# Second batch's first normalised x turned by transfers and VectorE block transposes; another order where the feed-forward begins; the last tile in two banks

## The reference, cut to what matters

```python
mod = (silu(c) @ wmod).reshape(2, 6, 1, -1)      # sa, ca, ga, sb, cb, gb
ga, gb = sign(g) * max(|g|, 0.25)                # for both gates
h = layernorm(x) * (1 + ca) + sa
x = x + ga * (h @ (weight * block_mask).T)       # 512 x 512, mask in 32 x 32 blocks
h = layernorm(x) * (1 + cb) + sb
inner = silu((h @ Wg.T) * ag) * ((h @ Wu.T) * au)   # 1376 wide
x = x + gb * ((inner @ Wd.T) * ad)
```

## Time and profile before

| | us |
|---|---|
| median of three runs | 180.3 |
| profiled execution, its own time | 180.65 |
| its span, first to last instruction | 178.5 |
| PE busy in the span | 170.8 |
| ACT, DVE, POOL busy | 82.0, 95.1, 29.6 |
| transfers | 22.93 MB |

### The profile page before, as it was taken

The page is one execution under the profiler, slowest core; times in us unless marked ns, Lnnn a source line. Parts: engine busy times, 40 slices in busy tenths (PEclk is TensorE's granted clock), DMA queues, the critical chain, the costliest instruction groups (busy, mean ns, idle before and its releaser), DMA issues.

```text
span 178.5 us, 2520 instructions
## 1 busy us (share of the span) xinstructions
PE 170.8 (96%) x893; PEld 129.6 (73%) x893; DVE 95.1 (53%) x194; ACT 82.0 (46%) x115; POOL 29.6 (17%) x40
## 2 busy tenths in 40 slices
PE   6979999999999999999999999999999999999990
PEld 6945545665458688788888888888888888888870
DVE  6882661483285798345455764327644223444493
ACT  3022213717979986833664444543335534242200
POOL 1443420292009330000000000005500000000000
PEclk9999999999999999999999999999999999999999
DMA  5999998999208700441300000001500000000033
GB/s 174 362 410 394 421 410 310 407 409 400 80 2 268 221 0 14 101 98 31 121 0 4 6 0 0 4 0 39 194 9 0 4 0 4 0 6 0 0 118 121
DMA packets 11668, 22.93 MB, mean 128 GB/s; under 512 B 2712, under 2 KB 4768, under 8 KB 11136
## 3 DMA queue, kind: packets, MB, share of 16 engines
q1 hardware_dynamic: 10528, 21.57, 33.3%
q10 hardware_dynamic: 1120, 1.07, 1.8%
HBM read 19.48 MB, written 2.10 MB: 121 GB/s over the span
## 4 chain that ended last, share of the span: by engine, by line
PE 86%; ACT 4%; DVE 3%; DMA 3%; issue 2%; SPq 1%; ACTq 0%
PE bank L771 45%; PE bank L825 23%; PE bank L741 12%; PE bank L685 3%; ACT junk L385 3%; PE bank L725 3%; DMA xt<-in_x 3%; DVE xn L485 1%; SPq L224 1%; ACT whi_gu L392 1%; PE bank L749 0%; DVE bns L466 0%; DVE xn L607 0%; DVE xt L672 0%; ACT hbuf L373 0%
## 5 line engine op out<-in xcount | busy, mean ns | idle before, releaser
L771 PE MATMUL bank<-ht,whi_gu 128*128 128x512 f32 x352 | 83.8, 391 | 0.3 <-issue 0.3
L771 PEld LDWEIGHTS bank<-ht,whi_gu 128*128 128x128 f32 x352 | 65.9, 188 | 15.0 <-issue 1.2
L588 DVE SCALAR_TENSOR_TENSOR awork<-bank,scal,awork 128x512 f32<-128x512 f32 x22 | 16.5, 751 | 51.2 <-PE bank L771 48.3
L825 PE MATMUL bank<-whi_dn,in_split 128*128 128x512 f32 x168 | 41.8, 390 | 0.0
L825 PEld LDWEIGHTS bank<-whi_dn,in_split 128*128 128x128 f32 x168 | 31.5, 188 | 6.5
L431 ACT ACTIVATE awork<-bank,scal 128x512 f32<-128x512 f32 x22 | 15.1, 688 | 43.5 <-PE bank L771 43.3
L741 PE MATMUL bank<-awork,wffn 128*128 128x512 f32 x64 | 31.3, 605 | 0.0
L392 ACT ACTIVATE whi_gu<-wffn 128x1024 fp32r<-128x1024 f32 x22 | 23.3, 1058 | 7.3 <-PE bank L771 7.3
L385 ACT ACTIVATE junk<-wffn 128x1536 uint8<-128x1536 uint16 x11 | 16.3, 1482 | 0.6
L741 PEld LDWEIGHTS bank<-awork,wffn 128*128 128x128 f32 x64 | 10.6, 190 | 7.6 <-issue 6.7
L597 DVE TENSOR_TENSOR in_split<-awork,in_split 128x512 fp32r<-128x512 f32 x21 | 15.5, 740 | 0.7
(11 more groups left out here) (61 smaller groups left out, 96.7 us busy)
## 6 DMA issues: line engine op xcount, KB each, us to landing
wffn<-in_w_gu SPq DMA_DIRECT2D x10, 512.0 KB, 8.2
wffn<-in_w_down SPq DMA_DIRECT2D x10, 256.0 KB, 9.0
xt<-in_x SPq DMA_DIRECT2D x8, 256.0 KB, 6.9
modw<-in_mod_ln SPq DMA_DIRECT2D x4, 512.0 KB, 7.2
modw<-in_mod_gate SPq DMA_DIRECT2D x2, 1024.0 KB, 8.8
modw<-in_mod_ln SPq DMA_DIRECT2D x2, 1024.0 KB, 11.0
maskt<-in_att_mask SPq DMA_DIRECT2D x4, 256.0 KB, 6.4
awork<-in_att_w SPq DMA_DIRECT2D x4, 256.0 KB, 7.3
```

The costliest lines, as they stand in the source:

```text
L588: dve.scalar_tensor_tensor(inner[:, s % 2, :], bank[gu_bank(s, 1)][:, :], scal[:, c, 1:2], silu_g[:, s % 2, :], ALU.mult, ALU.mult).then_i ...
L771: return pe.matmul(bank[gu_bank(s, u)][:, :], w, h, start=(k == 0 and part == 0), stop=(k == KT - 1 and part == 1))
L825: last = pe.matmul(bank[4 + t][:, :], h, w, start=(c == 0 and part == 0), stop=(c == C - 1 and part == 1))
```

## The change

- **Turned by transfers.** `xn` of q = 1 is normalised into space that later holds chunk 4 and 5, moved by 16 transfers (8 on SP, 8 on ACT; each 32 partitions x 2 KB), and turned by four DVE block transposes into `turned[0]`, in space of chunks 6 and 7; `modulate(4)` to `(7)` read it there. `transposes(4)` to `(7)` leave PE. SP puts its 8 transfers, and a wait for the normalised tile, ahead of chunk 0; chunk 4 waits for the moves and chunk 5 for `modulate(7)`. For q = 3 the 16 transfers become of the same new form.
- **Order before the linear of batch 1.** On DVE one `stats` goes ahead of `mod_columns(2)`, and the others and `normalise(1)` ahead of `mod_columns(3)`. On POOL `inverse_deviation(1, .)` goes ahead of `mask_weights(3)`, which waits for the normalised tile.
- **Order where the feed-forward begins.** `normalise(2)` before `mod_columns(4)`, `transposes(8)` to `(11)` one step earlier, checks and modulations mixed in another way, and two checks taken out of step 0.
- **The last tile.** In batch 1 the down product of tile 3 is made as two column halves of 256, in banks 7 and 3, each with its own gate, add and transfer out.

```diff
+TURN_CHUNK = H1_CHUNK - 4
+GRP = P // BLK
 LAG = 2
 HELD = 4
+HALF = D // 2
 SHIFT = BLK + NB
-CHECKS_AT = {0: 3, 2: 1, 3: 2}
+CHECKS_AT = {0: 1, 1: 1, 2: 1, 3: 2}
...
-        xq = modw[:, 0, :, :].rearrange("p t (j k c) -> p t j k c", j=P // BLK, k=KT)
-        xb = modw[:, 1, :, :].rearrange("p t (i k c) -> p t i k c", i=P // BLK, k=KT)
+        early = wffn[:, TURN_CHUNK:H1_CHUNK, :].rearrange("p c n -> p (c n)")
+        turn_from = [early[:, 0:TT * D].rearrange("p (j n) -> p j n", n=TT * P), modw[:, 0, :, :]]
+        turn_to = [early[:, TT * D:2 * TT * D].rearrange("p (i n) -> p i n", n=TT * P), modw[:, 1, :, :]]
+        turned = [early[:, 2 * TT * D:3 * TT * D].rearrange("p (k s) -> p k s", s=SEQ), xn]
...
+
+            def move_group(layer, i):
+                for j in range(GRP):
+                    sp.dma_start(turn_to[layer][BLK * j:BLK * (j + 1), i, :],
+                                 turn_from[layer][BLK * i:BLK * (i + 1), j, :]).then_inc(d_turn[layer][i], 16)
...
+            sp.wait_ge(xn_ok, 2 * TT)
+            for i in range(GRP // 2):
+                move_group(0, i)
             for c in range(C):
+                if c == TURN_CHUNK:
+                    for i in range(GRP):
+                        sp.wait_ge(d_turn[0][i], 16 * GRP)
+                if c == TURN_CHUNK + 1:
+                    sp.wait_ge(h_ok, 2 * TT)
...
-            for j in range(P // BLK):
-                for i in range(P // BLK):
-                    sp.dma_start(modw[BLK * j:BLK * (j + 1), 1, :, i * P:(i + 1) * P],
-                                 modw[BLK * i:BLK * (i + 1), 0, :, j * P:(j + 1) * P]).then_inc(d_blocks[j], 16)
+            for i in range(GRP):
+                move_group(1, i)
...
+                if k == KT - 1:
+                    pool.wait_ge(xn_ok, 2 * TT)
...
-            for k in range(KT):
+            for k in range(KT - 1):
                 mask_weights(k)
             inverse_deviation(1, 0)
             inverse_deviation(1, 1)
+            mask_weights(KT - 1)
...
-                src = bank[4 + n % 2][:, :] if q < 2 else bank[n % 2][:, :] if q == 2 else xn[:, k, :]
+                src = turned[layer][:, k, :] if b == 1 else bank[(4 if q == 0 else 0) + n % 2][:, :]
...
+            act.wait_ge(xn_ok, 2 * TT)
+            for i in range(GRP // 2, GRP):
+                for j in range(GRP):
+                    act.dma_start(turn_to[0][BLK * j:BLK * (j + 1), i, :],
+                                  turn_from[0][BLK * i:BLK * (i + 1), j, :]).then_inc(d_turn[0][i], 16)
...
+            for _ in range(3):
+                check_chunk(next(check_at))
+            copy_rows(5)
+            for _ in range(2):
+                check_chunk(next(check_at))
+            modulate(8)
+            modulate(9)
+            round_gu(0)
+            modulate(10)
+            modulate(11)
             check_chunk(next(check_at))
-            copy_rows(5)
-            for _ in range(4):
-                check_chunk(next(check_at))
-            round_gu(0)
-            for n in range(8, 12):
-                modulate(n)
...
-                if q:
+                if q == 2:
...
-                    if q == 3:
-                        dst = xq[:, t, :, :, :].rearrange("p j k c -> p k j c")
+                    if q % NB == 1:
+                        dst = turn_from[q // NB].rearrange("p j (t k c) -> p t k j c", t=TT, c=BLK)[:, t, :, :, :]
                         src = src.rearrange("p (k j c) -> p k j c", k=KT, c=BLK)
                     dve.tensor_scalar(dst, src, mv[:, q, t, 0:1], rstd[:, q, t:t + 1],
                                       ALU.subtract, ALU.mult).then_inc(xn_ok, 1)
-            def transpose_blocks(k):
-                for j in range(P // BLK):
-                    dve.wait_ge(d_blocks[j], 16 * (P // BLK))
-                dve.wait_ge(xt_done, 3 * TT)
-                dve.transpose(xn[:, k, :].rearrange("p (t i c) -> p t i c", t=TT, c=BLK), xb[:, :, :, k, :])\
+            def transpose_blocks(layer, k):
+                for i in range(GRP):
+                    dve.wait_ge(d_turn[layer][i], 16 * GRP)
+                dve.wait_ge(xt_done, TT * (NB * layer + 1))
+                dve.transpose(turned[layer][:, k, :].rearrange("p (t i c) -> p i t c", t=TT, c=BLK),
+                              turn_to[layer].rearrange("p i (t k c) -> p i t k c", t=TT, c=BLK)[:, :, :, k, :])\
...
-                dve.wait_ge(xt_done, TT * NB + TT * b)
+                dve.wait_ge(xt_done, 3 * TT if b else TT)
...
+            stats(1, 0)
             mod_columns(2)
             keep_blocks(3)
-            stats(1, 0)
             stats(1, 1)
             stats(1, 2)
-            mod_columns(3)
             stats(1, 3)
             normalise(1)
+            mod_columns(3)
             guard_gate(0)
+            for k in range(KT):
+                transpose_blocks(0, k)
             for t in range(TT):
                 gate_linear(0, t)
             for t in range(TT):
                 stats(2, t)
+            normalise(2)
             mod_columns(4)
-            normalise(2)
+            split(8)
             flag_vector(0)
+            split(9)
             read_flag(0)
-            for n in range(8, 12):
-                split(n)
+            split(10)
+            split(11)
...
-                    transpose_blocks(s - 5)
+                    transpose_blocks(1, s - 5)
                 if 6 <= s < 10:
                     split(6 + s)
                 if s == C + LAG - 1:
                     for t in range(TT):
                         gate_ffn(0, t)
-            for t in range(TT):
+            for t in range(TT - 1):
                 n = TT + t
                 gate_ffn(1, t)
-                if n >= BY_POOL:
-                    dve.wait_ge(acc_read, n + 1)
-                    dve.tensor_tensor(xt[:, n, :], xt[:, n, :], xn[:, t, :], ALU.add)\
-                       .then_inc(out_last, 1)
+                dve.wait_ge(acc_read, n + 1)
+                dve.tensor_tensor(xt[:, n, :], xt[:, n, :], xn[:, t, :], ALU.add)\
+                   .then_inc(out_last, 1)
+            n = NB * TT - 1
+            for i, src in enumerate((bank[7], bank[3])):
+                cols = slice(i * HALF, (i + 1) * HALF)
+                dve.wait_ge(half_mm, i + 1)
+                dve.scalar_tensor_tensor(xn[:, TT - 1, cols], src[:, cols], 2.0, gates[:, 3, cols],
+                                         ALU.mult, ALU.mult).then_inc(half_read, 1)
+                dve.wait_ge(half_read, i + 1)
+                dve.tensor_tensor(xt[:, n, cols], xt[:, n, cols], xn[:, TT - 1, cols], ALU.add)\
+                   .then_inc(out_last, 1)
...
-                dst = bank[4 + n % 2] if q < 2 else bank[n % 2]
+                dst = bank[(4 if q == 0 else 0) + n % 2]
...
-                        pe.wait_ge(h_ok, 7 + t)
+                        pe.wait_ge(h_ok, 3 + t)
...
+
+            def down_half(s, i, native):
+
+                c = s % C
+                cols = slice(i * HALF, (i + 1) * HALF)
+                for part in range(2):
+                    h = inner_part(s, part)[:, (TT - 1) * P:TT * P]
+                    w = whi_d(s)
+                    if native:
+                        h, w = h.bitcast(F32), raw_d(c)
+                    last = pe.matmul(bank[7 if i == 0 else 3][:, cols], h, w[:, cols],
+                                     start=(c == 0 and part == 0), stop=(c == C - 1 and part == 1))
+                if c == C - 1:
+                    last.then_inc(half_mm, 1)
+                elif i == 1 and s < STEPS - HELD:
+                    last.then_inc(down_mm, 1)
...
+                        pe.wait_ge(h_ok, 4 * TT)
+
+                def products(native):
+                    for t in range(TT - b):
+                        down_product(s, t, native)
+                    if b == 1:
+                        for i in range(2):
+                            down_half(s, i, native)
+
                 with pe.If(general[GROUP_OF[c]]):
-                    for t in range(TT):
-                        down_product(s, t, True)
+                    products(True)
                 with pe.Else():
-                    for t in range(TT):
-                        down_product(s, t, False)
+                    products(False)
...
-                    for t in (2, 3):
+                    for s in (o, p, a, z):
+                        down_product(s, 2, native)
+                    for i in range(2):
                         for s in (o, p, a, z):
-                            down_product(s, t, native)
+                            down_half(s, i, native)
...
-                (3, 0): [lambda: transposes(4), gate_columns],
-                (3, 1): [lambda: transposes(5)],
-                (3, 2): [lambda: gate_first(0), lambda: transposes(6)],
-                (3, 3): [lambda: transposes(7), lambda: gate_first(1)],
+                (3, 0): [gate_columns],
+                (3, 2): [lambda: gate_first(0)],
```

(20 more changed lines are left out.)

## The result

The changed kernel takes 183.5 us in the median of four runs (182.4 to 185.0), beside 181.2 for the kernel before on the same chip. The ratio is 1.017, 95% interval 1.012 to 1.022. The forecast was 179.5, range 178.0 to 181.8: wrong, and of the wrong sign.

A forecast was written before the change was run, and what follows sets the result against it. The prediction took PE, busy 170.8 of 178.5 us, as the bound, with transfers also full at the start. Its terms summed to -0.81 us from the profiled 180.65, giving 179.8, or 179.5 us for the median; range 178.0 to 181.8.

The forecast's parts named there:

- Transposes off PE, -1.76: Transposes 4 to 7 leave PE: four groups of 0.44 us on the chain, -1.76 us if nothing else is late.
- `stats` ahead of `mod_columns(2)`, +0.36: One `stats` earlier on DVE delays PE's mask sums, ending near 19.5 instead of 19.14: +0.36 us.
- A move's issue at 0.40 us: Each of the 16 moves takes 0.40 us to issue, ends 0.34 and 0.68; `copy_rows(4)` then costs nothing.
- The moves land 2.0 us after issue, at 29.8: Moves land at 29.8, so DVE's turns let `modulate(4)` end near 31.7, ahead of PE's need at 32.4.
- The second gate copy, +0.15: On ACT after `modulate(4)`, the second gate copy ends about 35.3, was 34.82; `linear(1, 0, 3)` waits: +0.15 us.
- Late weights, +1.05 at `copy_rows(5)`: Chunk 2 lands at 40.4; three checks ahead of `copy_rows(5)` delay PE's column transpose to near 42.55: +1.05 us.
- Behind it nothing else is late: After `copy_rows(5)`, checks 3 and 4 end at about 46 and modulation 8 at 46.9, ahead of transposes 10 at about 48.
- The slow-issue rival: Moves issue 0.68 us apart, PE waits at `copy_rows(4)`, `mod_gate[1]` and `copy_rows(5)`: +1.29, 181.6 us; chance 0.17.
- The order, -0.22 - 0.34: Where the feed-forward begins: transposes 10 regain 0.22 us, and the 0.34 us pause before step 2's gate matmuls goes.
- The halves at 0.120 us: Last tile's 44 half-width matmuls take 0.120 us each, against 22 full ones at 0.226: +0.3 us.
- The load-paced rival: Weight loads of 188 ns pace the halves in batch 1's down products: 3.3 us instead of 0.3, 182.5 us; chance 0.10.
- The tail, -0.35: At the kernel's end, half-wide DVE instructions and a transfer of half the bytes give -0.35 us (-0.1 to -0.8).

The follow-up runs named there:

- e6: Changed kernel without the first turn's 16 moves, block transposes reading the tile where it lies (batch 1 values wrong, only time counts): 177.6 us, ratio 0.985.
- e4: Changed kernel with 18 calls of an unused identity product put ahead of PE's stop, as filler: 183.8 us, ratio 1.015 to the kernel before.
- e9: Changed kernel with ACT's eight moves issued by POOL instead: 183.1 us, ratio 1.016 to the kernel before.
- e11: Changed kernel with `mod_ln2[1]` issued ahead of SP's moves and ACT's moves issued by POOL: 181.5 us, ratio 1.006 to the kernel before.
- e12: Changed kernel with `copy_rows(5)` behind one chunk check instead of three: 183.2 us, ratio 1.016 to the kernel before.
- e13: Kernel before with new last tile and feed-forward order, no moves, SP holding chunk 0 and all behind it until `modulate(4)` ended: 183.8 us, ratio 1.014.
- e2: Kernel before with only the new order where the feed-forward begins: 179.4 us, ratio 0.993.
- e8: Kernel before with both the split last tile and the new feed-forward order, no turn by transfers: 178.9 us, ratio 0.991.
- e3: Changed kernel without the new feed-forward order and without the halves, so the turn by transfers alone: 183.5 us, ratio 1.014 to the kernel before.
- e1: Kernel before with only the last tile in two banks, as column halves with the halved end: 179.9 us, ratio 0.995.
- e5: Changed kernel with chunk 0 and `mod_ln2[1]` issued ahead of SP's eight moves: 186.6 us, ratio 1.032 to the kernel before.
- e15: Changed kernel with `mod_ln2[1]` ahead and the moves split 4 on SP, 4 on ACT, 8 on POOL: 187.2 us, ratio 1.036 to the kernel before.

## Why the prediction was wrong, by its own steps

- **Transposes off PE, -1.76**: L773 has 32 matmuls and 32 loads, 16 fewer. Right; e6 shows the gain, 1.3 us net of the next term, where nothing else is late.
- **`stats` ahead of `mod_columns(2)`, +0.36**: right. The chain has 0.14 of issue and 0.38 for the mask sums where it had 0.13, +0.39.
- **The tile ready at 24.2**: it was 25.1, of which 0.5 is the x tile, landed at 18.3 instead of 17.8.
- **A move's issue at 0.40 us**: wrong. 0.600 on SP and 0.67 from one to the next, 0.614 on ACT: what the earlier trace rows had shown for the other form. One piece of 2 KB per partition costs the issuer what four of 512 B do. I took the nearest row by bytes; the nearest by kind, SBUF to SBUF over 32 partitions, was right. `copy_rows(4)` came at 31.5, where I had it end at 28.4, and PE stood 2.36 us.
- **The moves land 2.0 us after issue, at 29.8**: right for most (medians 2.0 and 2.1), wrong for the last, which took 3.8 with chunk 0 already issued. The turns began at 34.9, and `modulate(4)` ended near 36.4 instead of 31.7.
- **The second gate copy, +0.15**: PE waits 0.23 us for it in e4, e9, e11 and e12; no such wait shows in the changed kernel, where PE passes this place at the lower clock.
- **Late weights, +1.05 at `copy_rows(5)`**: the step that failed. That the weights would be late, and that this was the largest cost, was right; the size and the place of the term were wrong. e13 measures the lateness alone at 4.9 us. Chunk 0 went out at 30.56, not 27.4, which is 3.2 us. The rest is the way in which I counted landings: first byte 2 us after issue, then 407 GB/s until the bytes issued so far are in. By that sum chunk 4, with 6.0 MB up to it, would land at 47.4. It landed at 51.3, and `mod_gate[1]` at 42.0 (39.6 by the sum, 36.5 in the forecast). From 31.00 to 51.26 us the transfers ran at 379 GB/s, 7.7 MB, of which an estimated 0.2 are the last of the moves; so 1.4 MB of later chunks had passed, 3.5 us of the queue. The slow start (271 GB/s from 31 to 34) matters little beside that.
- **"Behind it nothing else is late"**: false, and with the step above the main error. I followed the late chunks only to chunk 2. The flag needs chunk 4 checked, and that ended at 52.9 where I had 46. e12 bears it out: with the wait that I had priced gone, the flag still comes late and the time is the same.
- **The slow-issue rival**, 181.6: its condition came true, and the measured median still lies 1.9 us above it, for the same reason.
- **The order, -0.22 - 0.34**: right in kind in e2 and e8, and too small: e2 gained 1.3 us by its ratio. In its chain all transposes add 0.44, and 48 gate matmuls in one piece 10.91 where it was 7.30 + 0.34 + 3.93. In the changed kernel the pause ahead of step 2 is gone too, but transposes still wait, 0.40 us at 53.58, and the start is later than in e3.
- **The halves at 0.120 us**: right. Four of them add 0.47 us, 0.118 each. The load-paced rival is out, and so is the estimate of 0.213 by the serial rule of the Trainium skill ("TensorE: Matmul & The Clock Gate", section "The mechanism") that stood beside it: in the trace each 256-column matmul has a 128-wide load, shown as 189 ns, and the pair adds 0.118 us.

```profile
132.29 3.65 PE bank L819 x16
135.94 1.36 PE bank L889 x6
137.30 0.47 PE bank L875 x4
```

- **The tail, -0.35**: the right sign, too small. From PE's last matmul, at 179.87 in the changed kernel, DVE takes 1.14 us instead of 1.44. I had given the transfer next to nothing; from DVE's end at 181.01 to the span's end it is 2.2 us, where it was 3.0 (the earlier trace rows end at 175.53, the span at 178.5). e1 has this part and the halves alone: -0.9 us in the medians (-0.4 to -1.5 by the interval), where the two terms of the sum make -0.05.

```profile
179.35 0.42 DVE L717 SCALAR_TENSOR_TENSOR xn<-bank,maskt 128x256 f32<-128x256 f32 x1
...
180.59 0.42 DVE L720 TENSOR_TENSOR xt<-xt,xn 128x256 f32<-128x256 f32 x1
```

## What to carry to other kernels

Where transfers run full, moving work from an engine to small transfers costs the queue twice: here they landed in time only in an empty queue, and while it was empty the bulk loads fell behind. Price the last load that anyone waits for, not the next one, and allow for loads issued behind it that share the queue. Ask what else in an issuing engine's order stands behind a new wait, and since when it could have gone. Take the issue time of a transfer from a row of the same kind (source, target, partitions) before one of the same size. Half-width matmuls cost PE next to nothing here (0.118 us each, 0.226 for a full one), and the split last tile ended the kernel 0.5% sooner.

## What the runs showed of the hardware that I had not expected

- Moves within SBUF load the transfer engines more than their bytes say: share 0.82 for 200 GB/s between 28 and 31 us, when the moves ran alone, where loads had 1.04 for 407. Per unit of share that is 244 against 391 GB/s.
- 64 KB among bulk loads landed after up to 7.4 us (e5) and 8.1 us (e15, issued by POOL), 2.0 in a free queue; issuing from another engine did not help.
- A queue that had run dry averaged 291 and 319 GB/s over its next two stretches of 3 us (e13), and a load's last piece landed after about 1 MB of loads issued behind it.
- PE stood 2.36 us, ran on, and was then granted 1.2 instead of 2.4 GHz for a while (mean 0.61 from 34 to 37 us). A stop of this length does not decide it: e12 had 2.35 us and kept 2.4, and so did e13 with a stop of 2.71 us.
